# A one-core decoder layer: experts' element work reordered, router weights by a tangent, one block of transposes moved

## The reference, cut to what matters

```python
x = x + attention(layernorm(x))              # 16 heads, causal
x = x + context_attention(layernorm(x))      # scores over 512 context tokens, masked
x = x + experts(layernorm(x))

# experts, x: (T, 256)
logits = x @ router_weight.T + router_bias               # (T, 16)
top_val, top_idx = top_k(logits, 4)
scores = zeros.at[top_idx].set(softmax(top_val))         # the other twelve are 0
gate_up = einsum('th,ehd->etd', x, gate_up_proj) + bias  # every expert, every token
gate = minimum(gate_up[..., ::2], 7.0)
up = clip(gate_up[..., 1::2], -7.0, 7.0)
glu = gate * sigmoid(1.702 * gate)
out = einsum('etd,edh->eth', (up + 1.0) * glu, down_proj) + down_bias
out = (out * scores.T[:, :, None]).sum(axis=0)
```

## Time and profile before

| What | Value |
|---|---|
| median of three runs | 227.85 us |
| the profiled execution's own time | 227.91 us |
| its span, first to last instruction | 225.8 us |
| granted TensorE clock, mean | 1.000 |
| TensorE matmul busy | 215.7 us, 96% |
| VectorE busy | 176.1 us, 78% |
| ScalarE busy | 125.6 us, 56% |
| GpSimd busy | 84.3 us, 37% |
| matmuls L1155 (128x512) | 360, mean 389 to 392 ns |
| matmuls L1171 (128x256) | 360, mean 283 to 294 ns |

### The profile page before, as it was taken

The page is one execution under the profiler, slowest core; times in us unless marked ns, Lnnn a source line. Parts: engine busy times, 40 slices in busy tenths (PEclk is TensorE's granted clock), DMA queues, the critical chain, the costliest instruction groups (busy, mean ns, idle before and its releaser), DMA issues. The chain is left out here.

```text
span 225.8 us, 4387 instructions
## 1 busy us (share of the span) xinstructions
PE 215.7 (96%) x1394; PEld 175.9 (78%) x1394; DVE 176.1 (78%) x433; ACT 125.6 (56%) x248; POOL 84.3 (37%) x70
## 2 busy tenths in 40 slices
PE   7999999998997998899999999999999999999995
PEld 2688767776685987698797888888888887887894
DVE  3579887777768546888979879879879889889865
ACT  2239789778533219266466476385384484484540
POOL 6359989001011010443444435435426426425000
PEclk9999999999999999999999999999999999999999
DMA  6894420000000000040340340430421422310002
GB/s 181 328 378 140 141 86 0 0 4 0 3 0 0 3 0 1 0 142 20 122 129 12 139 126 17 139 101 38 139 77 62 139 64 75 139 46 0 0 0 93
DMA packets 7997, 17.41 MB, mean 77 GB/s; under 512 B 928, under 2 KB 3120, under 8 KB 7856
## 3 DMA queue, kind: packets, MB, share of 16 engines
q1 hardware_dynamic: 7552, 16.94, 22.9%
q10 hardware_dynamic: 432, 0.31, 0.4%
HBM read 16.72 MB, written 0.52 MB: 76 GB/s over the span
## 5 line engine op out<-in xcount | busy, mean ns | idle before, releaser
L307 POOL TENSOR_TENSOR WLg<-raw_g,WHg 128x1024 fp32r<-128x1024 f32 x16 | 38.3, 2394 | 49.8 <-ACT WHg L407 49.6
L837 DVE SCALAR_TENSOR_TENSOR pt<-pt 128x512 f32<-128x512 f32 x30 | 49.4, 1648 | 4.2 <-DVE pt L833 1.8
L536 ACT ACTIVATE HH<-pt 128x512 fp32r<-128x512 f32 x30 | 19.0, 632 | 53.1 <-DVE pt L837 53.0
L1155 PE MATMUL PS<-XH,WHg 128*128 128x512 f32 x120 | 47.0, 392 | 0.7 <-ACT pt L527 0.7
L1155 PE MATMUL PS<-XL,WHg 128*128 128x512 f32 x120 | 46.9, 391 | 0.0
L1155 PE MATMUL PS<-XH,WLg 128*128 128x512 f32 x120 | 46.7, 389 | 0.0
L1171 PE MATMUL PS<-WHd,HH 128*128 128x256 f32 x120 | 35.3, 294 | 1.5 <-DVE HL L842 1.1
L1171 PE MATMUL PS<-WLd,HH 128*128 128x256 f32 x120 | 33.9, 283 | 0.0
L1171 PE MATMUL PS<-WHd,HL 128*128 128x256 f32 x120 | 33.9, 283 | 0.0
L842 DVE TENSOR_TENSOR HL<-pt,HH 128x512 fp32r<-128x512 f32 x30 | 22.2, 739 | 11.0 <-ACT HH L536 11.0
L314 POOL TENSOR_TENSOR WLd<-raw_w,WHd 128x512 fp32r<-128x512 f32 x15 | 19.7, 1315 | 28.4 <-ACT WHd L413 28.3
(11 more groups left out here) (157 smaller groups left out, 349.2 us busy)
## 6 DMA issues: line engine op xcount, KB each, us to landing
raw_g<-we_d SPq DMA_DIRECT2D x16, 512.0 KB, 4.0
raw_w<-we_d SPq DMA_DIRECT2D x16, 256.0 KB, 2.7
ctxT<-ctxT_d SPq DMA_DIRECT2D x1, 1024.0 KB, 10.0
ctx_sb<-ctx_d SPq DMA_DIRECT2D x1, 1024.0 KB, 12.1
wqkv<-wqkv_d SPq DMA_DIRECT2D x3, 256.0 KB, 5.0
out_d<-x SPq DMA_DIRECT2D x4, 128.0 KB, 1.8
rows<-rows_d SPq DMA_DIRECT2D x1, 264.0 KB, 6.3
x<-x_d ACTq DMA_DIRECT2D x2, 128.0 KB, 3.2
```

The source lines that it names most:

```text
L307: g.tensor_tensor(WLg[slot][:, :, :, :].rearrange("p k g f -> p (k g f)"), raw_g[slot][:, :], WHg[slot][:, :, :, :].rearrange("p k g f -> ...
L536: a.activation(HH[slot][:, m, :], hid[:, m, :], ACT.Copy).then_inc(hh_done, 1)
L837: v_.scalar_tensor_tensor(out=hid[:, m, :], in0=glu[:, m, :], scalar=GLU_MAX, in1=upc[:, m, :], op0=ALU.min, op1=ALU.mult).then_inc(hid_do ...
L1155: i = t.matmul(PS[:, 2 * m + part, :], w[slot][:, k, part, m * P:(m + 1) * P], xx[:, k, :], start=(n == 0), stop=(n == 3 * KD - 1))
```

## The change

Four edits:

1. In each expert's body, VectorE does both products first, then both low parts, then all four weighted sums (before: product, low part, product, two sums, low part, two sums). In body 0 the copy of the transposed scores moves from before the first low part to behind it.
2. In each expert's body ScalarE makes both high parts of the hidden values before the high part of the next weights (before: the weights' copy stood between the two).
3. The router's exponentials are made from a hyperbolic tangent, exp(d) = ((1 + tanh(d/8)) / (1 - tanh(d/8)))^4, with the division and the two squarings on VectorE; and ScalarE's table of functions for the gelu is requested behind the first `high_tokens` of the third layernorm.
4. TensorE transposes the normalised values of chunks 0 and 1 between the two `context_turn`s of chunks 2 and 3 and not behind both; ScalarE takes both turned chunks before it copies the high part.

```diff
@@ scalar: end of context attention, router
             context_take(2)
+            context_take(3)
             high_tokens(0, 9, slice(0, S), xh_done)
-            context_take(3)
+            a.preload_act_table_set("gelu_apprx_sigmoid_and_others")
             act.wait_ge(xs_done, NC)
             high_tokens(6, 10, slice(S, S + P), xh_done)
             high_tokens(4, 11, slice(S + P, T), xh_done)
             act.wait_ge(dlog_done, 1)
-            a.activation(elog[:, :, :], dlog[:, :, :], ACT.Exp).then_inc(elog_done, 1)
+            a.activation(elog[:, :, :], dlog[:, :, :], ACT.Tanh, scale=0.125).then_inc(elog_done, 1)
@@ scalar: body of an expert
                 take(0)
                 take(1)
                 high(0)
+                high(1)
                 if not isinstance(e, int) or e + 2 < E:
                     high_gate_up(e + 2, slot, pair + 1)
-                high(1)
                 if not isinstance(e, int) or e + 1 < LAST:
                     high_down(e + 1, 1 - slot, pair + slot)
@@ vector: router
             link(i)
+            dve.wait_ge(elog_done, 1)
+            v_.tensor_scalar(root[:, :, :], elog[:, :, :], -1.0, 1.0, ALU.mult, ALU.add)
             link(v_.tensor_tensor(within[:, :, :], rank[:, :, :], need[:, :].unsqueeze(2).to_broadcast([P, NC, E]), ALU.is_le))
+            v_.reciprocal(esel[:, :, :], root[:, :, :])
             link(v_.tensor_tensor(sel_eq[:, :, :], eq[:, :, :], within[:, :, :], ALU.mult))
+            v_.scalar_tensor_tensor(out=root[:, :, :], in0=elog[:, :, :], scalar=1.0, in1=esel[:, :, :], op0=ALU.add, op1=ALU.mult)
             link(v_.tensor_tensor(sel[:, :, :], sel_eq[:, :, :], gt[:, :, :], ALU.add))
-            dve.wait_ge(elog_done, 1)
+            link(v_.tensor_tensor(esel[:, :, :], root[:, :, :], root[:, :, :], ALU.mult))
+            link(v_.tensor_tensor(elog[:, :, :], esel[:, :, :], esel[:, :, :], ALU.mult))
             link(v_.tensor_tensor(esel[:, :, :], elog[:, :, :], sel[:, :, :], ALU.mult))
@@ vector: body of an expert
                 product(0)
+                product(1)
+                low(0)
                 if isinstance(e, int) and e == 0:
                     dve.wait_ge(scoreT_ps, 1)
                     v_.tensor_copy(scoreT[:, :], PS[0:E, 5, :]).then_inc(scoreT_done, 1)
-                low(0)
-                product(1)
-                if isinstance(e, int) and e == 0:
                     low(1)
 ...
                 else:
-                    weighted_sum(e - 1, 1 - slot, (0, 1))
                     low(1)
-                    weighted_sum(e - 1, 1 - slot, (2, 3))
+                    weighted_sum(e - 1, 1 - slot, range(NC))
@@ tensor
             context_turn(2)
+            transposes(xn, 0, 0, xn_done, NC + 3 * QC)
             context_turn(3)
-            transposes(xn, 0, 0, xn_done, NC + 3 * QC)
             context_values(2)
```

More of the change, by code:

```diff
@@ L133, in decoder_layer @@
         elog = sb("elog", [P, NC, E])
+        root = sb("root", [P, NC, E])
         esel = sb("esel", [P, NC, E])
```

## The result

The changed kernel takes 221.81 us (median of four, 221.69 to 222.23) against 227.91 in the same runs (227.73 to 228.24): the ratio is 0.9734, with a 95% interval of 0.9716 to 0.9752. The forecast was 221.4, the range 220.7 to 223.6. The profiled execution took 221.69 us with a span of 219.6; its mean granted clock is 1.000, as before.

What follows compares the result with a forecast made beforehand. It took the expert loop to be bound by a ScalarE, GpSimd and VectorE ring, not TensorE. Gains 4.2 + 0.40 + 0.92 + 0.9 = 6.4 us off 227.91 give 221.5, median 221.4; range 220.7 to 223.6.

Steps and rivals of the forecast that it cites:

- a ring of ScalarE, GpSimd and VectorE: Expert loop: element work on these engines, without TensorE, sets the round at 8.62 us; removing that bound gains 4.2 us.
- the hold for the gelu: Before the experts: TensorE waits 0.92 us for the first gelu behind the table load; the early load gains 0.92 us.
- the transposes: Context turns of chunks 2 and 3: four transposes fill TensorE's wait for ScalarE's exponential; gain 0.40 us.
- the first body: Start of the experts, up to `down(0)`: the new order gains 1.07 - 0.16 = 0.9 us.
- The hold: Before the second matmul of `down(0)`: TensorE came 1.07 us late because the first low part was slowed by GpSimd.
- five microseconds of slack: Expert loop after the change: the hidden values' low parts are done five microseconds before `down` needs them.
- what remains as a ring is ScalarE's: Expert loop after the change: the only remaining ring is ScalarE's own work, 5.8 us, under TensorE's 8.32.
- a product may still meet WLd: Expert loop: GpSimd's low part of the down weights (1.3 us) may block a VectorE product; five microseconds cover it.
- Rival (c): Expert loop: the weights' chain becomes the ring, with rounds of 9.1 us; 231.6 us in total, chance 0.05.
- (a): Seam from `gate_up` to `down` in the loop: its 0.32 us is TensorE's own; 225.2 us, chance 0.11.
- (b): Router: the tangent isn't in the gelu's table, so two loads of 1.28 us are needed; 223.4 us, chance 0.05.
- (d): Whole kernel: TensorE's rate falls as the other engines bunch, and eats the gain; chance 0.02.

Runs made afterwards that it cites:

- e1: The kernel before with only the new VectorE and ScalarE orders in the expert bodies; 223.01 us.
- e2: The changed kernel with both expert bodies in the old order, keeping only the tangent, early table load and moved transposes; 227.49 us.
- e5: The kernel before with GpSimd's subtraction for the low part of the gate/up weights cut to half its columns, experts 2 to 15; 223.35 us.
- a2: The changed kernel with the transposes of chunks 0 and 1 behind both turns again, high part of the tokens between the takes; 222.04 us.
- a4: The changed kernel with half a pass more of GpSimd's gate/up weight subtraction, experts 2 to 15; 225.41 us.
- e3: The kernel before with ScalarE's new order alone; 227.56 us.
- e4: The kernel before with VectorE's new order alone; 223.10 us.
- b3: The kernel before with GpSimd's gate/up weight subtraction done twice, experts 2 to 15; 246.45 us.

## Why the prediction was right, and where it was not

**The bound.** Right, and shown by e1, e2 and e5: the loop was bound by a ring of ScalarE, GpSimd and VectorE, and TensorE at 96% busy followed it. The gain by rounds is 120.70 - 116.75 = 3.95 us where 4.2 was forecast; the term was sized with a round of 8.32, and it is 8.34.

**The start.** At the second matmul of `gate_up(1)` the changed kernel is 87.25 - 85.88 = 1.37 us ahead, forecast 1.32 (0.40 + 0.92); 0.14 of that was there before any edit, at the turn of chunk 2 (71.66 and 71.52). Of the rest, the hold for the gelu gave 0.91, forecast 0.92, which leaves 0.32 to the transposes where 0.40 was forecast; the start of the turned block gained more (0.44, a2), and 0.1 of it was lost again behind it. At the second of `down(0)` it is 96.09 - 93.81 = 2.28 ahead, so the first body gave 0.91, forecast 0.9. That this fits is luck, for two terms were off and cancel. The hold was sized at 1.07 us, but from the last matmul of `gate_up(1)` to the second of `down(0)` it went from 3.34 us (96.09 - 92.75) to 2.47 (93.81 - 91.34), which is 0.87. And the biases lost nothing to the copy of the scores, where 0.16 was charged: they start 0.32 us behind that last matmul, as they do in e1, where the copy had ended 2 us before. The reciprocal, taken from its growth per column as 0.54 us, took 0.56. The margin of the low part ahead of WLg, forecast 0.55 us, was 0.58. The 2.28 and the 3.95 add up to the 6.2 us between the two profiled executions.

**The steps that failed**, though the time came out in the range. First, "five microseconds of slack" and "what remains as a ring is ScalarE's ... 5.8 us". The due times were right (second product at the end of `gate_up` plus 1.95, in the trace 154.31 - 152.23 = 2.08; WLg's end at plus 6.1, in the trace 6.27), but they hold only while TensorE paces. The ring that takes over when it doesn't runs through both of GpSimd's passes and is about 7.3 us long, so the cover is about 1.0 us (a4, e3). I had seen that "a product may still meet WLd" and did not put it into the ring. Rival (c) had this mechanism; its 9.1 us put the four takes in series with GpSimd, and they run beside it. At 7.3 us it is 1.0 us short of the point at which it decides. Second, both orders were credited with the loop; VectorE's alone does it (e4), and ScalarE's alone leaves a round of 8.7 us (e3).

**The rivals.** (a) is out by e2's seams of 0.34 and 0.63 in one loop, and by e5. (b) is out: one load in the trace, at 74.69, none between the tangent and the gelu, so the set named for the gelu serves the tangent too. (c) did not decide: the rounds are 8.34. (d) is out: 5.47 us for 24 matmuls of 128x512 before and after.

## What to carry to other kernels

A busy share of 96% doesn't make an engine the bound: compare the distance between starts at a seam where the inputs had been ready for long with the same distance in the loop, and look whether the engine starts at a constant distance behind another one's end. Where VectorE and GpSimd both read SBUF, put the one's instructions that others wait for ahead of what releases the other's long pass, and let the block fall on work with slack. Measure that slack by lengthening the pass, for the times at which things are due tell only the slack in the present pace, not the length of the ring that takes over.

## What the runs showed of the hardware that I had not expected

GpSimd's pass is stretched too where the two engines meet. WLd takes 1.29 us in the changed kernel's round, but 1.47 in e3 and 1.48 in a4. It follows WLg directly in all three, but in e3 and a4 a VectorE clip that WLg had blocked gets through at the handover: in a4 it ends at 157.15, 0.29 us behind WLg's end, and the product behind it is blocked again until WLd is done. So two GpSimd passes back to back do not block VectorE as one long pass would; this is also why b3's round grew by 1.3 us and not by 2.4.

The clip has one tensor input in SBUF and not two, and it is blocked all the same: 1.33 us in the changed kernel and 2.52 in a4, where a free one takes 0.43. The weighted sums, with one of their inputs in PSUM, are not: in the changed kernel the four take 1.65 us from 155.62, beside WLg.

In one execution a hold of TensorE also went with a fall of its clock. In e2 TensorE waited for the low part from 93.8 to 95.4 us of the span, and the granted clock fell to 0.50 at about 94.3 and stayed there until 101. With the 0.81 us of idle time at this place before the change it stayed at 1.00 in the profiled execution, and in the changed kernel, which has none, it was 1.00 from 80 to 200 us.
